# A two-layer graph network on one core: all five indirect passes with 128 rows in each transfer

## The reference

```python
h = relu(layernorm(x))
x = x + spline_conv(h)   # sum over edges of basis(e) x h[src] x weight[9], over degree, + h @ root_w.T + root_b
h = relu(layernorm(x))
x = x + gat_block(h)     # 8 heads: softmax over the edges of a dst and the node itself; then LN, 32->128->32, LN
```

## Time and profile before

| | |
|---|---|
| median of three runs | 3,093.12 us |
| the profiled execution | 3,089.18 us, its span 3,087.3 us |
| busy: PE, DVE, ACT, POOL | 69%, 58%, 28%, 80% |
| mean granted clock of TensorE | 0.812 |
| software queue (indirect transfers) | 64,000 packets, 30.57 MB |
| hardware queue (loads and stores by SP) | 52,070 packets, 91.52 MB |

### The profile page before, as it was taken

How to read it: one execution, slowest core, us unless ns; L and a number is a source line. 1 busy time by engine, 2 the same in 40 slices (tenths; PEclk the granted TensorE clock), 3 DMA queues, 4 the chain that set the end, 5 groups by cost and what they waited for, 6 DMA issues and landing times.

```text
span 3087.3 us, 33471 instructions
## 1 busy us (share of the span) xinstructions
PE 2138.2 (69%) x10666; PEld 1492.6 (48%) x10666; DVE 1802.5 (58%) x3234; ACT 852.1 (28%) x1616; POOL 2468.6 (80%) x2011
## 2 busy tenths in 40 slices
PE   2777787756888878878887804876466877689710
PEld 1555555534666656556665503654333544355400
DVE  4889898995444444444444402444657689898600
ACT  1322233313333333333333302332111233123300
POOL 7777777777788888878788777788878888887877
PEclk9988898977878888888888856787577877899755
DMA  2333333331221222222121111111111111111100
GB/s 61 80 73 79 75 72 73 67 75 19 42 42 33 40 44 48 40 45 45 38 42 34 34 17 18 32 33 27 41 12 11 24 25 37 11 40 32 23 10 10
DMA packets 116219, 123.99 MB, mean 40 GB/s; under 512 B 70726, under 2 KB 72747, under 8 KB 116070
## 3 DMA queue, kind: packets, MB, share of 16 engines
q0 software_dynamic: 64000, 30.57, 10.6%
q1 hardware_dynamic: 52070, 91.52, 9.3%
HBM read 59.51 MB, written 64.00 MB: 40 GB/s over the span
## 4 chain that ended last, share of the span: by engine, by line
POOL 74%; issue 19%; DVE 4%; PE 2%; DMA 1%; POOLq 0%; ACT 0%; DVEq 0%
POOL ring L460 42%; POOL out_rows L508 16%; POOL x_table L482 16%; DVE region L1383 1%; PE V L598 1%; DVE region L1375 1%; DVE region L1311 0%; DVE region L1323 0%; PE T L525 0%; DMA ring<-in_x,index 0%; PE C L540 0%; DVE region L1320 0%; DMA ring<-x_table,index 0%; PE T L590 0%; DVE var L1280 0%
## 5 line engine op out<-in xcount | busy, mean ns | idle before, releaser
L460 POOL DMA_INDIRECT ring<-in_x,index x800 | 980.5, 1226 | 244.3 <-issue 244.0
L1280 DVE TENSOR_REDUCE var<-sq 125x16 f32<-125x512 f32 x325 | 221.4, 681 | 734.2 <-ACT sq L960 733.5
L508 POOL DMA_INDIRECT out_rows<-region,scatter_to x400 | 502.6, 1256 | 121.9 <-issue 121.9
L460 POOL DMA_INDIRECT ring<-x_table,index x400 | 496.3, 1241 | 124.4 <-issue 124.1
L482 POOL DMA_INDIRECT x_table<-region,index_out x400 | 486.3, 1216 | 124.4 <-issue 121.6
L564 PE MATMUL V<-xT,w_q 128*128 128x500 f32 x600 | 370.1, 755 | 25.1 <-ACT xT L952 24.0
L960 ACT ACTIVATE sq<-C 125x512 f32<-125x512 f32 x300 | 178.8, 596 | 729.0 <-PE C L576 422.4
L540 PE MATMUL C<-center,xT 128*125 128x128 f32 x1400 | 230.2, 317 | 90.0 <-ACT xT L952 47.8
L598 PE MATMUL V<-region,hT 128*125 128x384 f32 x600 | 255.3, 541 | 42.7 <-DVE region L1375 42.7
L540 PEld LDWEIGHTS C<-center,xT 128*125 128x125 f32 x1400 | 210.2, 224 | 154.3 <-issue 111.5
L576 PEld LDWEIGHTS C<-w_c,hid 128*125 128x125 f32 x2400 | 278.5, 195 | 0.0
(11 more groups left out here) (251 smaller groups left out, 3230.9 us busy)
## 6 DMA issues: line engine op xcount, KB each, us to landing
ring<-in_x,index POOLq DMA_INDIRECT x800, 3.1
nodes<-in_x SPq DMA_DIRECT2D x25, 500.0 KB
x_table<-nodes SPq DMA_DIRECT2D x25, 500.0 KB
x_plain<-nodes SPq DMA_DIRECT2D x25, 500.0 KB
nodes<-x_plain SPq DMA_DIRECT2D x50, 250.0 KB
out_rows<-nodes SPq DMA_DIRECT2D x50, 250.0 KB
x_table<-region,index_out POOLq DMA_INDIRECT x400, 2.6
ring<-x_table,index POOLq DMA_INDIRECT x400, 2.7
```

The lines of the kernel that those rows point to most:

```text
L460: pool.indirect_dma_start(out=ring[0:P, j, s * F:(s + 1) * F], out_offset=None, in_=table, in_offset=bass.IndirectOffsetOnAxis(ap=index[0: ...
L508: pool.indirect_dma_start(out=out[:, :], out_offset=bass.IndirectOffsetOnAxis(ap=scatter_to[0:P, e:e + 1], axis=0), in_=diff[0:P, e * F:(e ...
L1280: v.tensor_reduce(unit(var, k), slots(squares(k)), AX.X, ALU.add).then_inc(var_ready, 1)
```

## The change

Every indirect transfer now names 128 partitions (`ROWS`) in place of 125. The three more rows get numbers beyond the bound: DVE sets partitions 96 to 127 of `index` and `index_out` to N = 100,000 ahead of everything (`scatter_to` has numbers from N up in these partitions from its iota), and the gathers get the bounds check that the scatters have. SP waits with its first index loads for these memsets, since they cover partitions 96 to 124 too. What a skipped row would be read from or written to is filled: partitions 125 to 127 of `ring` with root_b (this load replaces the one for partition 125 at the end, comes first on SP, and POOL waits for it before the first gather), those of `region1` with rows of x (`surplus_in`, loaded between stages A and B, waited for before pass 5), and those of a part of `region2` with zeros.

```diff
+ROWS = 128
-N_BOOT = 6 * 4 + 2 + 2 + 2 + 4
+N_BOOT = 6 * 4 + 2 + 2 + 2 + 3
@@ SP, start @@
+            sp.dma_start(ring[P:ROWS, :, :].rearrange("a j (s f) -> a (j s) f", f=F),
+                         root_b.rearrange("(a b f) -> a b f", a=1, b=1).to_broadcast([ROWS - P, NJ * CE, F])).then_inc(root_b_in, 16)
+            sp.wait_ge(index_set, 2)
             for j in range(NJ):
                 index_load(src, 0, j, None)
...
-            load(ring[P:P + 1, :, :].rearrange("a j (s f) -> a (j s) f", f=F),
-                 root_b.rearrange("(a b f) -> a b f", a=1, b=1).to_broadcast([1, NJ * CE, F]))
@@ SP, behind stage A @@
+            sp.dma_start(region1[P:ROWS, :], x_rows[0:ROWS - P, 0:TE * F]).then_inc(surplus_in, 16)
@@ POOL @@
                     pool.indirect_dma_start(
-                        out=ring[0:P, j, s * F:(s + 1) * F], out_offset=None, in_=table,
-                        in_offset=bass.IndirectOffsetOnAxis(ap=index[0:P, j, s:s + 1], axis=0)).then_inc(ring_dma[j], 16)
+                        out=ring[0:ROWS, j, s * F:(s + 1) * F], out_offset=None, in_=table,
+                        in_offset=bass.IndirectOffsetOnAxis(ap=index[0:ROWS, j, s:s + 1], axis=0),
+                        bounds_check=last_row, oob_is_err=False).then_inc(ring_dma[j], 16)
+            pool.wait_ge(root_b_in, 16)
             gather_phase(x[:, :], 0, 0)
...
-                        out=x1_table[:, :], out_offset=bass.IndirectOffsetOnAxis(ap=index_out[0:P, j, s:s + 1], axis=0),
-                        in_=rows_out[0:P, j, s * F:(s + 1) * F], in_offset=None,
+                        out=x1_table[:, :], out_offset=bass.IndirectOffsetOnAxis(ap=index_out[0:ROWS, j, s:s + 1], axis=0),
+                        in_=rows_out[0:ROWS, j, s * F:(s + 1) * F], in_offset=None,
...
+            pool.wait_ge(surplus_in, 16)
...
-                        out=out[:, :], out_offset=bass.IndirectOffsetOnAxis(ap=scatter_to[0:P, e:e + 1], axis=0),
-                        in_=diff[0:P, e * F:(e + 1) * F], in_offset=None,
+                        out=out[:, :], out_offset=bass.IndirectOffsetOnAxis(ap=scatter_to[0:ROWS, e:e + 1], axis=0),
+                        in_=diff[0:ROWS, e * F:(e + 1) * F], in_offset=None,
@@ DVE, its first instructions @@
+            v.memset(index[96:ROWS, :, :], N).then_inc(index_set, 1)
+            v.memset(index_out[96:ROWS, :, :], N).then_inc(index_set, 1)
+            v.memset(region2[96:ROWS, 5904 + KS * GF:2 * H * TE + NJ * W], 0.0)
```

More of the change, by code:

```diff
@@ L276, in gnn_program @@
         msgs_done = sem("msgs_done")
+        index_set = sem("index_set"); root_b_in = sem("root_b_in"); surplus_in = sem("surplus_in")
         block = ctx.enter_context(nc.Block())
```

## The result

The changed kernel takes 2,882.56 us, the median of four runs (2,876.51 to 2,886.34), beside 3,092.68 us for the kernel before, measured with it (four runs, 3,090.3 to 3,096.14). The ratio is 0.9316, 95% interval 0.9305 to 0.9327: 210 us less. The forecast was 2,778 us, 105 us too low; the range 2,700 to 2,990 holds the result, the forecast case by itself (2,700 to 2,817) doesn't. The profiled execution took 2,886.34 us, its span 2,884.5 us.

What follows compares the result with a forecast made beforehand. POOL, issuing 2,000 indirect transfers without pause at about 1.54 us each, was taken as the bound. At 1.31 us the three stages ended at 2,757 us; 15 us of reserve gave span 2,772, time 2,778 us, range 2,700 to 2,990.

Steps and rivals of the forecast that it cites:

- the forecast case: All indirect transfers: with 128 rows split evenly over 16 engines each takes 0.42 to 1.0 us; time 2,700 to 2,817, chance 0.62.
- the small parts: Start-up wait for root_b, index loads behind memsets, the long memset and the surplus load: 0 to 3 us in all.
- The second stage: Scatter of x1 beside gathers by dst: compute-bound, POOL waits for x1_ready, from 673 us to the third pass at 1,706 us.
- rival (a): Fixed part of each transfer dominates, 1.00 to 1.15 us; POOL bounds throughout from 1.05 us; time 2,817 to 2,985, chance 0.21.
- signs of being wrong: Transfer medians at or above 1.19 us; or below 1.0 us with PE waiting as long as before and time above 2,850 us.
- (b): Rival: nothing changes, because the filler is not what takes a transfer's time; 3,093 to 3,099 us, chance 0.06.
- (c): Rival: slower, the generator goes row by row, 0.029 us more per transfer plus the start-up wait; 3,151 to 3,161 us, chance 0.11.
- the stage gains 65 us: Gathers of x and products: PE's 64.9 us of waits for rows vanish, first scatter moves from 737.7 to 673 us.
- tenth taken back: 15 us added to the span, a tenth of 156 us of removed PE waits, for the next engine's lateness.
- the bounds check that the gathers get costs nothing by these rows: Check added to gathers: at most 0.03 us, judged from scatters with it (1.189 us) against gathers without (1.209 us).
- the pace of 1.31 us: POOL's time per indirect transfer: 0.95 us for itself, 0.30 us of "issue", 0.05 us for longer ones among the last 800.
- the third stage: Gather of x1, then final scatter: 800 transfers at 1.31 us, 1,048 us, POOL ending last at 2,754, span 2,757 us.

Runs made afterwards that it cites:

- all125: Changed kernel with 125 rows in place of 128 in every transfer, all waits, loads, memsets and bounds checks kept; 3,163.88 us, ratio 1.0231.
- less_dve_again: Changed kernel without `total_block`, VectorE's reversed sums over a block (49 us of its work), an unchanged repeat on chip 1; 2,822.23 us, ratio 0.9117.
- before_less_dve: Kernel before without `total_block`, VectorE's reversed sums over a block (49 us of its work); 3,093.5 us, ratio 0.9993.
- check125: Kernel before with the bounds check added to its 1,200 gathers, 125 rows as before, nothing else; 3,169.24 us, ratio 1.0237.
- nocheck128: Changed kernel without the bounds check on gathers, the three surplus numbers 0 instead of N; 4,335.85 us, ratio 1.4001.
- sizes: Changed kernel with the final scatter's number of rows varied from chunk to chunk, 16 to 128; one execution, 2,968.31 us, only durations used.
- pass45_125: Changed kernel with 125 rows in the fourth and fifth pass alone (gathers of x1, final scatter), on chip 4; 3,946.49 us, ratio 1.2737.
- after_less_dve: Changed kernel without `total_block`, VectorE's reversed sums over a block (49 us of its work), on chip 4; 4,103.1 us, ratio 1.3287.
- pass45_again: Unchanged repeat on chip 1 of the changed kernel with 125 rows in the fourth and fifth pass alone; 3,027.87 us, ratio 0.9781.

## Why the prediction came out as it did

**Right.** POOL's descriptor writing was the bound, and the uneven split its cause: median 1.00 us where 0.95 was taken, "issue" unchanged, the filler gone, POOL waiting tens of microseconds for `x1_ready` (156.6 us), 128 rows in every pass worth their place. The first gather moved by 1.7 us, within the 0 to 10 taken, and `all125` bears out that the small parts cost next to nothing. The second stage took 1,043 us against 1,033. By its time the run lies among those of rival (a), by its mechanism it is the forecast case: (a) at its fast end, 1.00 us, still gave 2,817, and a POOL that bounds throughout was not seen. One of the prediction's signs of being wrong came true as well, a time above 2,850 us with TensorE waiting as long as before in the first stage. Rivals (b) and (c) fell: durations changed by a sixth, and downwards.

**Wrong: "the stage gains 65 us".** This step failed; the first stage gained 15 us (737.7 to 722.6), and 49.6 of the 112.5 us that the span is above its forecast come from it. The prediction had the row that speaks against it, DVE's 588.7 us of 688, and used it only as a bound on busy time. VectorE has 585.7 us of work up to 722 us: 88% of those 665 us, and the rest it stands behind the others. A wait of TensorE for rows and a wait of TensorE for VectorE overlapped: while TensorE waited for rows, VectorE caught up. VectorE's sums over a block of five chunks now come 119.5 us apart in place of 121.8 on average (316.4 to 435.9 us; three blocks from 208.5 to 573.9 us before), and the wait changed its name. The rows of the kernel before could have told it: VectorE's 99 us of idle time up to 745 us hold 89 us in which it waits for TensorE and ScalarE, 44.6 of them in the row above, so that little was left for a faster POOL to give. The "tenth taken back" (15 us) was the right thought, far too small. `less_dve_again`, with `before_less_dve` as its counterpart, shows that VectorE bounds the stage.

**Wrong: "the bounds check that the gathers get costs nothing by these rows".** The rows compared a scatter with a gather, which differ in more than the check. By `check125` it costs 0.064 us, 75 to 78 us over 1,200 gathers of 125 rows, and 0.054 us at 128 rows by `nocheck128`. Of the changed kernel's 65 us most lie in the first two stages, where POOL waits anyway; 400 x 0.054 = 22 us lie in the third, where it counts.

**Mis-sized: the pace of 1.31 us.** In the third stage it is (416.7 + 123.9 + 426.7 + 122.4)/800 = 1.362 us, and one wait of 23.4 us comes on top: 0.05 of it is the gather's and 0.03 the scatter's median above 0.95, on average 0.04, and 0.06 in place of 0.05 are the long ones. That is 800 x 0.052 = 42 us. With the wait of 23.4 us, not foreseen because compute was taken to be ahead of the last pass, it is 65 us; 5 us more stand behind POOL's last record (8.1 us to the end of the span, 3.0 us before), which nothing in the trace explains: the last packets moved within a microsecond. They go with the size of the last transfers: 8.1 to 8.2 us in every kernel that ends with 128 rows, 3.0 to 3.3 us in every one that ends with 125 or 127. Less the reserve of 15 us, and less the 2.3 us of idle time ahead of the first gather, which are the second stage's, that is the third term, 53 us.

Compute in this stage went from 1,082.5 us to 2,801.5 - 1,787.9 = 1,013.6 us, 69 of the 91 us of waits for rows; 23.8 us of them remain:

```profile
PE T L532 <- DMA ring<-x_table,index: 23.8, 9, 5.3
```

**Why the range held.** Its upper part belonged to rival (a), and so stood for every slower sum, whatever its cause. That the result fell into it is luck, since the three steps above, and not the mechanism of (a), made it slower. Two small slips of the working change nothing: its 1.204 us as the mean of today's medians is 1.201, and its low end of 2,706 us is 2,711 with the 5.8 us added. Of the Trainium skill's sentence that descriptor generation is small (DMA: Bandwidth & Descriptors, "Anatomy of one DMA - SWDGE (gpsimd) path") this kernel bears out nothing: it costs 0.84 to 2.55 us in `sizes`.

## To carry to other kernels

Look at the number of rows in every indirect transfer as at a divisor: name a multiple of 16, filled up with skipped numbers, rather than a prime or 5 x 25; and count the bounds check that the fill needs. When one engine's waits for data are to go, don't subtract them from the stage: see how busy the next engine is in that stage (here 86%), and give the stage no more than what is left above it, less what its own waits for the other engines take (here 99 - 89 = 10 us; the stage gained 15). And measure such a change on more than one chip.

## What the runs showed of the hardware that was not expected

**Waits that no work explains, on two chips.** `pass45_125` and `after_less_dve` first ran on one chip, `nocheck128` on another. All took 900 to 1,500 us more than reckoned, in each of four executions:

| kernel | first chip | time, us | another chip | time, us |
|---|---|---|---|---|
| `pass45_125` | 4 | 3,946.49 (3,936.69 to 3,952.57) | 1 (`pass45_again`) | 3,027.87 |
| `after_less_dve` | 4 | 4,103.1 (4,098.61 to 4,134.71) | 1 (`less_dve_again`) | 2,822.23 |
| `nocheck128` | 14 | 4,335.85 (4,327.06 to 4,345.1) | not run | |
| kernel before | 4, 14 | 3,095.13, 3,094.51 | 1 | 3,094.66 |

Their ratios were 1.2737 (1.2708 to 1.2766) and 1.3287 (1.3231 to 1.3344) for the first two. Kernels whose transfers all have 125 rows ran on the same two chips undisturbed, in turns with them: the kernel before, `before_less_dve` and `check125`. Two stretches of `pass45_125` and `pass45_again`, the same program, in the columns of the earlier trace rows:

```profile
57.00:600.00 543.00, 279.47 (x1286) 191.74 (x1287) 290.09 (x508) 105.42 (x204) 266.08 (x267) 0.83 0.17 46
```

```profile
57.00:600.00 543.00, 426.43 (x2161) 295.09 (x2160) 487.22 (x837) 174.75 (x337) 406.04 (x408) 0.92 0.28 75
```

In the same time the disturbed run gets through 60% of the instructions. The duration of a POOL transfer is no longer (median 0.997 us in both). What is late is releases between compute engines: the trace puts 1,119 us of waits in `pass45_125` down to "remote", 1,769 in `after_less_dve`, 1,869 in `nocheck128`, and none in any other run. The largest such group of `pass45_125`, then three rows of it in order of time (all engines):

```profile
ACT sq L967 <- remote: 508.1, 57, 26.6
```

```profile
324.11 1.14 PE L547 MATMUL C<-center,xT 128*125 128x128 f32 x8 [3.21 <-issue]
...
335.60 0.60 ACT L967 ACTIVATE sq<-C 125x512 f32<-125x512 f32 x1 [11.54 <-remote]
...
2685.28 1.28 POOL L464 DMA_INDIRECT ring<-x_table,index  x1 [3.46 <-issue]
```

TensorE's last matmul into `C` ends at 325.3 us and ScalarE begins with it at 335.6 us. The disturbance goes with the 128-row transfers inside one kernel too. The last row above is POOL's first gather of x1, and here is the same in `pass45_again`.

```profile
1760.65 1.28 POOL L464 DMA_INDIRECT ring<-x_table,index  x1 [3.33 <-issue]
```

Up to there, with 128 rows, the disturbed run is 924.6 us behind. From there on, with 125 rows, it takes 3,950.8 - 2,685.3 = 1,265.5 us and the other 3,026.5 - 1,760.7 = 1,265.8 us: the same. In `after_less_dve`, where this stage has 128 rows too, it takes 4,096.8 - 2,627.9 = 1,468.9 us, with 663 us of waits put down to "remote" in it, against 2,822.2 - 1,701.0 = 1,121.2 us in `less_dve_again`. What holds the releases back isn't settled. The number of the chip of the changed kernel's first measurement (2,882.56 us) isn't on record, the second (2,877.65 us) was on chip 1; no run shows it on a chip where the others were disturbed, so whether its gain of 210 us exists there is open. The five kernels with 128-row transfers that ran on chip 1 or on chip 7 weren't disturbed.

**The fixed price of an indirect transfer.** With the 0.30 us between two of them it is about 1.15 us, so that a transfer of 16 rows, 0.84 + 0.30 us, costs 89% of one of 128, 0.98 + 0.30 us.
